# Products of probabilities and V in the tiles of the scores: two batches a product, and outputs that share two banks with the turned q and k

## The reference, cut to what matters

```python
scale, shift = split(emb @ W_emb + b_emb)
xn = rms_norm(x, g_norm) * (1.0 + scale) + shift
q, k, v = heads(xn @ W_qkv)                 # 16 heads of 16 channels, 32 positions
q = rms_norm(q, g_q);  k = rms_norm(k, g_k)
attn = softmax(q @ k^T * 16 ** -0.5)        # 32 x 32 for each batch and head
o = attn @ v                                # the product that the change touches
x = x + (o + o @ W_out)
x = x + GRU(initial = cond, inputs = x)     # 32 steps, one after the other
```

## Time and profile before

| | |
|---|---|
| time, median of 3 runs | 345.14 us (343.35 to 345.91) |
| the profiled execution | 347.7 us, of which its span is 345.5 us |
| mean granted TensorE clock | 0.995 |
| stretch of 18 even turns of the attention | 65.4 to 156.4 us of the span |
| the GRU's steps | from about 198 us to the end |

### The profile page before, as it was taken

How to read it: one execution, slowest core, us unless ns; L and a number is a source line. 1 busy time by engine, 2 the same in 40 slices (tenths; PEclk the granted TensorE clock), 3 DMA queues, 4 the chain that set the end, 5 groups by cost and what they waited for, 6 DMA issues and landing times.

```text
span 345.5 us, 12266 instructions
## 1 busy us (share of the span) xinstructions
PE 327.8 (95%) x4182; PEld 296.1 (86%) x4182; DVE 251.4 (73%) x665; ACT 237.3 (69%) x721; POOL 224.2 (65%) x403
## 2 busy tenths in 40 slices
PE   8998879999999999999976999999999999999994
PEld 7767667888888888888865999999999999999994
DVE  2768859999999999999987366655556566665555
ACT  3778767788787888888655566666666666666662
POOL 5688667687787778779965345555555555555552
PEclk9999989999999999999999999999999999999999
DMA  6885644334333332333342221121111111111111
GB/s 198 288 250 145 187 137 138 94 81 122 117 115 95 118 102 80 116 115 104 110 121 69 68 71 47 61 64 61 61 51 56 46 60 61 61 61 61 61 59 35
DMA packets 32199, 34.06 MB, mean 99 GB/s; under 512 B 5286, under 2 KB 26796, under 8 KB 32172
## 3 DMA queue, kind: packets, MB, share of 16 engines
q1 hardware_dynamic: 26108, 26.30, 25.4%
q10 hardware_dynamic: 6064, 7.41, 6.7%
HBM read 12.46 MB, written 8.39 MB: 60 GB/s over the span
## 4 chain that ended last, share of the span: by engine, by line
PE 82%; SPq 8%; ACT 2%; DVE 2%; DMA 2%; issue 2%; POOL 1%; DVEq 0%; POOLq 0%; ACTq 0%
PE bank L1206 38%; PE bank L1163 20%; PE bank L1336 5%; PE bank L1317 4%; SPq L394 4%; PE bank L1305 4%; SPq L402 4%; PE bank L1436 3%; PE bank L1169 2%; DMA operands<-operands 2%; PE bank L1288 2%; PE bank L1297 2%; PE bank L1183 1%; PE bank L1246 0%; DVE probsT L1042 0%
## 5 line engine op out<-in xcount | busy, mean ns | idle before, releaser
L1206 PE MATMUL bank<-wih_lo,wo_parts 128*128 128x256 f32 x192 | 56.3, 294 | 0.0
L1206 PE MATMUL bank<-wih_hi,wo_parts 128*128 128x256 f32 x192 | 53.7, 281 | 0.0
L1206 PE MATMUL bank<-wih_hi,pair_lo 128*128 128x256 f32 x192 | 52.9, 280 | 0.0
L1206 PE MATMUL bank<-wqkv_hi,hT_hi 128*128 128x256 f32 x192 | 52.7, 293 | 0.0
L583 POOL TENSOR_TENSOR operands<-operands,h 128x128 f32<-128x128 f32 x64 | 29.6, 462 | 35.4 <-ACT operands L869 34.4
L1206 PE MATMUL bank<-wqkv_lo,hT_hi 128*128 128x256 f32 x192 | 50.1, 280 | 0.0
L1106 DVE TENSOR_TENSOR operands<-bank,operands 128x128 f32<-128x128 f32 x64 | 18.6, 291 | 39.8 <-ACT operands L866 39.8
L1163 PE MATMUL bank<-wqkv_hi,xn_hi 128*128 128x512 f32 (+1 forms) x124 | 46.6, 376 | 0.3 <-POOL xn_lo L505 0.3
L1206 PE MATMUL bank<-wqkv_hi,hT_lo 128*128 128x256 f32 x192 | 42.8, 279 | 0.0
L590 POOL TENSOR_TENSOR w_emb_sb<-h,w_emb_sb 128x256 f32<-128x256 f32 x31 | 22.7, 733 | 30.0 <-DVE h L1123 30.0
L1163 PE MATMUL bank<-wqkv_hi,xn_lo 128*128 128x512 f32 (+1 forms) x124 | 42.0, 338 | 0.0
(11 more groups left out here) (136 smaller groups left out, 984.7 us busy)
## 6 DMA issues: line engine op xcount, KB each, us to landing
v_diag<-v_rows SPq DMA_DIRECT2D x128, 34.0 KB, 1.9
operands<-operands SPq DMA_DIRECT2D x64, 64.0 KB, 2.0
operands<-operands SPq DMA_DIRECT2D x32, 128.0 KB, 2.1
out_dram<-x ACTq DMA_DIRECT2D x16, 256.0 KB, 2.5
w_emb_sb<-out_dram SPq DMA_DIRECT2D x32, 128.0 KB, 2.1
out_dram<-w_emb_sb SPq DMA_DIRECT2D x31, 128.0 KB, 1.7
x_in<-in_x_dram SPq DMA_DIRECT2D x7, 512.0 KB, 9.0
stage_w<-in_L_cond_W_ih_dram ACTq DMA_DIRECT2D x2, 384.0 KB, 4.8
```

Of the source, the lines that this page charges most:

```text
L1206: return pe.matmul(dst, moved, gate_columns(weights, k, block), start=False, stop=True, skip_group_check=True)
```

## The change

The products of probabilities and V are cut into the tiles of the scores: 64 rows by 32 columns, two batches in each, so 32 products of 34 columns in place of 16 of 68. Row half i writes to `o_tiles[i]`, and the two are in different banks. To find a second bank for them, the outputs share two banks (`p_ko`) with the turned q and k: each bank holds one half of the turned q and k in its first 256 columns and the outputs of two batches behind them. Since ScalarE copies the turned q and k out of the banks from which VectorE reads the outputs, `reciprocals` now also waits until `queries_keys` of the group that was turned in the same TensorE turn is done (`qkT_ready`), and `attention_products` waits for the copy of the turn before. The readers' access patterns get one dimension more (the bank). The GRU's gate banks move accordingly: reset and update gates of the odd steps to `p_ko`, new gates to the two banks of the scores; so the new gate's bank of step 0 is cleared, set and filled one turn later than the others.

```diff
--- before.py
+++ after.py
@@ -157,14 +157,19 @@
 
         r_g, z_g, rh, npre, n_g, zh, zn = (gru_tile(KC, P) for _ in range(7))
 
-        p_xTw, p_vx2, p_qkT = (bank(f"bank{i}") for i in range(3))
-        p_s = ctx.enter_context(nc.psum_tensor("bank3", [P, 2 * BANK], F32))
-        p_o = bank("bank5")
+        p_xTw, p_vx2 = (bank(f"bank{i}") for i in range(2))
+        p_ko = ctx.enter_context(nc.psum_tensor("bank2", [P, 2 * BANK], F32))
+        p_s = ctx.enter_context(nc.psum_tensor("bank4", [P, 2 * BANK], F32))
         p_qk2 = ctx.enter_context(nc.psum_tensor("bank6", [P, 2 * BANK], F32))
         p_qk = [p_qk2[:, BANK * i:BANK * i + BANK] for i in range(2)]
         p_xT, p_w = p_xTw[:, 0:D], p_xTw[:, D:2 * D]
         p_x2T, p_v = p_vx2[:, 0:D], p_vx2[:, D:2 * D]
         s_tiles = [p_s[:, BANK * i:BANK * i + D] for i in range(2)]
+        OW = GB // 2 * (HEADS // 4) * VW
+        qkT_tiles = [p_ko[:, BANK * i:BANK * i + D] for i in range(2)]
+        qkT_halves = p_ko[:, :].rearrange("p (i f) -> p i f", i=2)[:, :, 0:D]
+        o_tiles = [p_ko[:, BANK * i + D:BANK * i + D + OW] for i in range(2)]
+        o_heads = p_ko[:, :].rearrange("p (i f) -> p i f", i=2)[:, :, D:D + OW].rearrange("p i (n f) -> p i n f", f=VW)
         s_heads = p_s[:, :].rearrange("p (i f) -> p i f", i=2)[:, :, 0:D].rearrange("p i (h k) -> p i h k", k=T)
 
 
@@ -237,6 +242,7 @@
         k_masked_ready = sem("k_masked_ready")
         k_diag_ready = [sem("k_diag_ready0"), sem("k_diag_ready1")]
         scores_clear = sem("scores_clear")
+        outputs_clear = sem("outputs_clear")
         square_x_free = sem("square_x_free")
         xhat_free = sem("xhat_free")
         s_ps = sem("s_ps")
@@ -326,8 +332,8 @@
 
 
 
-        rz_banks = [p.rearrange("p (c f) -> p c f", c=KC)[:, :, 0:2 * P] for p in (p_qk2[:, :], p_s[:, :])]
-        n_banks = [p_qkT, p_o]
+        rz_banks = [p.rearrange("p (c f) -> p c f", c=KC)[:, :, 0:2 * P] for p in (p_qk2[:, :], p_ko[:, :])]
+        n_banks = [p_s[:, BANK * i:BANK * i + BANK] for i in range(2)]
         hT_banks = [p_xTw[:, 0:P], p_vx2[:, 0:P]]
 
         def pair_index(base, n):
@@ -628,7 +634,7 @@
             act.wait_ge(qk_loaded[0], 16)
             act.copy(wqkv_hi[:, 0, 0:2 * D], stage_w[:, 0, 0:2 * D]).then_inc(wqk_hi_ready[0], 1)
             act.wait_ge(vec_ps, 1)
-            act.copy(vec_cols[:, :], p_o[:, 0:8]).then_inc(vec_cols_ready, 1)
+            act.copy(vec_cols[:, :], p_ko[:, 0:8]).then_inc(vec_cols_ready, 1)
 
             def shifts():
                 act.wait_ge(vec_cols_ready, 1)
@@ -686,9 +692,15 @@
                 for c in range(KC):
                     act.copy(hT_hi[:, c, :], condT[:, c, :]).then_inc(hi_ready[c], 1)
 
+            def set_reset_update(e):
+                act.copy(rz_banks[e].rearrange("p c (g a) -> p c g a", g=2), bias_sum).then_inc(rz_set, 1)
+
+            def set_new(e):
+                act.copy(n_banks[e].rearrange("p (i f) -> p i f", i=2), bias_n).then_inc(n_set, 1)
+
             def set_gates(e):
-                act.copy(rz_banks[e].rearrange("p c (g a) -> p c g a", g=2), bias_sum).then_inc(rz_set, 1)
-                act.copy(n_banks[e].rearrange("p (i f) -> p i f", i=2), bias_n).then_inc(n_set, 1)
+                set_reset_update(e)
+                set_new(e)
 
             def roots(n, nslot):
                 lo, hi = norm_columns(n)
@@ -723,7 +735,7 @@
                 if later(g, 2):
                     act.wait_ge(k_masked_ready, g - 1)
                     act.wait_ge(s_ps, g - 1)
-                act.copy(qkT[:, slot, :], p_qkT[:, :]).then_inc(qkT_ready, 1)
+                act.copy(qkT[:, slot, :].rearrange("p (i f) -> p i f", i=2), qkT_halves).then_inc(qkT_ready, 1)
 
             def exponentials(g, slot):
                 act.wait_ge(logits_ready, g + 1)
@@ -835,7 +847,10 @@
                 if turn_is(base, u, NG - 3 + ACT_OT):
                     act.wait_ge(bias_ready, 1)
                     act.wait_ge(gates_clear[0], 1)
-                    set_gates(0)
+                    set_reset_update(0)
+                if turn_is(base, u, NG - 2 + ACT_OT):
+                    act.wait_ge(gates_clear[0], 2)
+                    set_new(0)
 
             pipeline(act, body, NG - 1 + ACT_X2T)
 
@@ -1005,16 +1020,17 @@
                                   .broadcast_to([P, 2, HEADS // 2, T]),
                                   ALU.subtract).then_inc(logits_ready, 1)
 
-            o_heads = p_o[:, 0:GB * HEADS // 4 * VW].rearrange("p (n f) -> p n f", f=VW)
-
             def reciprocals(o, slot):
                 dve.wait_ge(o_ps, o + 1)
-                dve.reciprocal(inv_sum[:, slot, :], o_heads[:, :, DH]).then_inc(inv_ready, 1)
+                dve.wait_ge(qkT_ready, capped(o, PE_PV - PE_QKT + 1))
+                dve.reciprocal(inv_sum[:, slot, :].rearrange("p (i n) -> p i n", i=2), o_heads[:, :, :, DH])\
+                   .then_inc(inv_ready, 1)
 
             def attention_output(o, slot):
                 dve.wait_ge(inv_ready, o + 1)
-                dve.tensor_tensor(o_sb[:, slot, :].rearrange("p (n d) -> p n d", d=DH), o_heads[:, :, 0:DH],
-                                  inv_sum[:, slot, :].unsqueeze(2).broadcast_to([P, HEADS, DH]),
+                dve.tensor_tensor(o_sb[:, slot, :].rearrange("p (i n d) -> p i n d", i=2, d=DH), o_heads[:, :, :, 0:DH],
+                                  inv_sum[:, slot, :].rearrange("p (i n) -> p i n", i=2).unsqueeze(3)
+                                  .broadcast_to([P, 2, HEADS // 2, DH]),
                                   ALU.mult).then_inc(o_ready, 1)
 
             def modulated(g, slot):
@@ -1185,7 +1201,7 @@
                                          start=c == 0, stop=c == KC - 1)
                 last.then_inc(emb_ps, 1)
             pe.wait_ge(vec_loaded, 16 * 4)
-            pe.transpose(p_o[:, 0:8], vec_rows[:, :], ident[0:8, 0:8]).then_inc(vec_ps, 1)
+            pe.transpose(p_ko[:, 0:8], vec_rows[:, :], ident[0:8, 0:8]).then_inc(vec_ps, 1)
             keep_busy(p_qk[1], 12)
 
             def projection_input(slot):
@@ -1302,7 +1318,7 @@
                 if later(g, 1):
                     pe.wait_ge(qkT_ready, g)
                 for m in range(2 * KC):
-                    last = pe.transpose(p_qkT[:, m * P:m * P + P], qkn[:, slot, m * P:m * P + P], ident[:, :])
+                    last = pe.transpose(qkT_tiles[m // KC][:, m % KC * P:m % KC * P + P], qkn[:, slot, m * P:m * P + P], ident[:, :])
                 last.then_inc(qkT_ps, 1)
 
             def scores(g, slot):
@@ -1323,18 +1339,22 @@
             def attention_products(g, slot, place):
                 pe.wait_ge(probsT_ready, g + 1)
                 pe.wait_ge(v_diag_ready[place], spread_by_four(g, place, GB))
+                pe.wait_ge(qkT_ready, capped(g, PE_PV - PE_QKT))
                 if later(g, 1):
                     pe.wait_ge(o_ready, g)
+                pe.sem_inc(outputs_clear, 1)
                 for hq in range(HEADS // 4):
                     for j in range(4):
 
                         c, e = hq // 2, hq % 2
                         head = HC * c + 2 * j + e
                         column = HC * (j // 2) + NB * c + 2 * e + (0, 1, 1, 0)[j]
-                        dst = p_o[32 * j:32 * j + 32, 0:GB * HEADS // 4 * VW]\
-                            .rearrange("p (b n f) -> p b n f", b=GB, f=VW)[:, :, hq, :]
-                        last = pe.matmul(dst, probsT[:, slot, column, :], v_diag[:, place, :, head, :],
-                                         start=True, stop=True)
+                        for i in range(2):
+                            rows = slice(2 * PB * i, 2 * PB * i + 2 * PB)
+                            dst = o_tiles[i][32 * j:32 * j + 32, :]\
+                                .rearrange("p (b n f) -> p b n f", b=GB // 2, f=VW)[:, :, hq, :]
+                            last = pe.matmul(dst, probsT[rows, slot, column, :],
+                                             v_diag[rows, place, 2 * i:2 * i + 2, head, :], start=True, stop=True)
                 last.then_inc(o_ps, 1)
 
             def output_projection(g, slot):
@@ -1384,16 +1404,21 @@
                 if turn_is(base, u, NG + PE_QKT):
                     pe.wait_ge(qkn_ready, NG)
                     pe.wait_ge(qkT_ready, NG)
-                    unread_products([rz_banks[0][:, 0, :], rz_banks[0][:, 1, :]], 3)
-                    clear_gates(0).then_inc(gates_clear[0], 1)
+                    unread_products([rz_banks[0][:, 0, :], rz_banks[0][:, 1, :]], 4)
+                    unread_products([rz_banks[0][:, 0, :], rz_banks[0][:, 1, :]], 2).then_inc(gates_clear[0], 1)
+                if turn_is(base, u, NG + 1 + PE_QKT):
+                    pe.wait_ge(logits_ready, NG)
+                    unread_products([n_banks[0][:, :]], 1).then_inc(gates_clear[0], 1)
                 if turn_is(base, u, NG + 2 + PE_QKT):
                     pe.wait_ge(rz_set, 1)
+                    for k in range(KC):
```

(9 more changed lines are left out.)

## The result

The changed kernel takes 353.52 us (median of 4 runs, 353.23 to 353.85) where the kernel before takes 345.14 (4 runs, 343.35 to 345.91). The ratio is 1.0236, with an interval from 1.0208 to 1.0263. The forecast was 344.3 and its range ended at 349.3. The profiled execution of the changed kernel took 353.36, with a span of 351.1. Two executions of this study (350.09 us of the kernel before and 354.15 of the run "cut in the loop alone") fell in a slower state, and no ratio uses them.

The account below looks back on a forecast made before the run. TensorE was taken as the bound, VectorE less than 0.35 us behind. Even turns -1.0, entry +0.3 and end -0.15 made -0.85 us, so 345.14 became 344.3, range 341.3 to 349.3.

Parts of the forecast that it names:

- eight starts at 7 ns take 0.053, so the starts set the pace: 64 x 6.7 ns = 0.43 us: TensorE's 32 small products: 64 records start at the pace seen over eight starts, 0.43 us in all.
- the 13 that the forecast had named as the sign of being wrong: TensorE's small products: 13 ns a record in the changed kernel would show the forecast wrong.
- The other bound, 27 ns a product: TensorE's small products at the pace of the scores' whole group: 0.87 us for 32, a turn 0.24 longer.
- rival 2: TensorE's small products are issued no faster than the scores' products: 0.24 us more a turn, 350 us; chance 0.13.
- The ring: VectorE's sum of squares, ScalarE's roots and copies, VectorE's `reciprocals` onward, closed by the new wait: 5.00 us a turn.
- sum of squares to the end of the copy: From the start of VectorE's sum of squares to the end of ScalarE's copy: 10.06 us over four turns.
- signal to `reciprocals`: Hand-over from ScalarE's copy to VectorE: 0.05 us a turn, bounds 0 to 0.12.
- `reciprocals` to `modulated`: On VectorE, from the start of `reciprocals` to that of `modulated`: 0.20 us a turn.
- `modulated` to the next sum: On VectorE, from `modulated` to the next sum of squares: 8.87 us over four turns.
- TensorE idle in every turn: Even turns: TensorE has idle time for the first time, some 0.15 us a turn.
- +0.3 and -0.15: Outside the 18 even turns: 0.3 us lost at the loop's entry before them, 0.15 us gained behind them.
- falls away after the last turned group: Behind the even turns, from 156 us on: the wait for the copy ends after the last turned group.

Follow-up runs that it names:

- cut in the loop alone: Kernel before with each of the 16 products cut in two on the same tile and bank, only in the loop's 20 turns: 348.89 us, ratio 1.0081.
- half the products: Changed kernel with 16 of its 32 products, two of four batches left out for each head from the second group on: 346.79 us, ratio 1.0034.
- the wait in the loop alone: Kernel before with `reciprocals` also waiting for ScalarE's copy of q and k, only in the loop's 20 turns: 347.50 us, ratio 1.0056.
- the wait alone: Kernel before with only one addition, `reciprocals` of every group also waiting for ScalarE's copy of q and k: 348.58 us, ratio 1.0103.
- the second profile of before: Kernel before run once more, unchanged, for another profile: 345.22 us.
- the products first: Changed kernel with ScalarE's store behind its copy of q and k, and TensorE's products with V ahead of the scores: 352.30 us, ratio 1.0179.

## Why the prediction was wrong

**The pace of the products.** The step that failed is "eight starts at 7 ns take 0.053, so the starts set the pace: 64 x 6.7 ns = 0.43 us", and with it "Eight starts at 7 ns speak for the fast end, and I take it". The starts 7 ns apart are real, and up to 32 records go out so fast behind long instructions. They are not sustained: 0.78 us for 64 behind the scores, and 0.75 with half the columns. That is 12 ns a record, near the 13 that the forecast had named as the sign of being wrong. The other bound, 27 ns a product from the group of scores, was near (24). It was the only pace that the trace of before showed over a whole group, and I set it aside for one seen over eight records. In TensorE's turn it makes +0.16 for -0.20 (+0.13 with the mean of 0.75), which decides the sign: rival 2 is what happened, at a chance of 0.13, and its own sum of 350 was still too low, because beside the longer turn it gave the wait 0.3 us at the loop's entry and no more. The rule of the Trainium skill named there ("TensorEngine Tiling (Array Packing)", section Instruction Overhead), that a short matmul costs as much as one of some 60 columns, gave an estimate of 0.80; behind the scores the trace agrees (0.78, and 0.75 with half the columns) if a product, and not each of its two records, is counted as a matmul, and behind long instructions it does not for the first 16 products (0.17 us).

**The ring.** The mechanism was right: `reciprocals` waits for the copy in every turn, the idle time moved there, and the store's turn is the latest. Its sizes were low. The run with half the products allows the comparison term by term over four turns (sums of squares at 94.87, 100.24, 105.17, 110.27 and 115.19; the rows above show one of these turns, the same two views have the others):

| term, four turns | forecast | measured |
|---|---|---|
| sum of squares to the end of the copy | 10.06 | 2.79 + 2.33 + 2.51 + 2.33 = 9.96 |
| signal to `reciprocals` | 0.20 | 0.09 + 3 x 0.10 = 0.39 |
| `reciprocals` to `modulated` | 0.80 | 0.28 + 0.22 + 0.28 + 0.28 = 1.06 |
| `modulated` to the next sum | 8.87 | 2.21 + 2.28 + 2.21 + 2.21 = 8.91 |
| together | 19.93 | 20.32 |

20.32 is 5.08 a turn, more than the old 5.055. So with the products as fast as I had them the kernel comes to about 346.8 (346.3 by its ratio to the runs of before beside it) and not to 344.3. The two terms that no row of before showed for this place, the signal and the start of `modulated` behind `reciprocals`, are the ones that were short. I had taken both nearer to their low ends than to their high ones: 0.05 of 0 to 0.12, and 0.20 of 0.16 to 0.37.

**Where the two are together.** In the changed kernel TensorE's 5.21 sets three turns of four, and the store's turn takes 5.58 (95.47 to 101.05): four turns are 21.18 for 20.22. The forecast had TensorE idle in every turn; it is idle in one of four.

**Ahead of and behind the even turns.** The forecast had +0.3 and -0.15; it was +1.6 and +2.5. I had written that the wait "falls away after the last turned group"; it still stands for the groups before, in turns with less work on TensorE, and the run with the wait in the loop alone has 1.5 less than the wait alone from group 25 to group 31. "The last products gain some 0.1" fell with the pace: they lost. In the changed kernel the products of group 31, the last, start 4.64 us after its scores, in the second profile of before 3.96. Which part of these 4 us is the products, which the wait, and which the longer code or SyncE's issues (10% of the chain for 8%) was not separated: the differences are near the 1 us by which unchanged stretches differ.

**What stays open.** That the number of small products sets their time, and not their columns, is shown, and that a first group of them goes out faster behind long instructions or after a wait. What sets the pace behind it, the fetching of instructions, their decoding or the weight load that each product has, was not tried. Nor was any run made with the shared banks or the readers' extra dimension alone; the run with half the products bounds them only together with the wait.

## What to carry to other kernels

Price small products by the pace of a whole group behind the same kind of work, never by the distances inside a burst; halving the columns of products of 68 columns while doubling their number was a loss here (0.46 us became 0.67 on the same tiles). A wait that joins two engines' chains has to be summed turn by turn with every hand-over in it (here 0.10 for a signal, and 0.28 to the next instruction), and here it decided in the one turn of four in which something else stood ahead of the signal: moving a store's issue behind the copy took 1.4 us of the wait's 1.7 in the loop. Cut a profile into stretches and profile the kernel before twice; the 18 looped turns agreed to 0.02 us, the start only to 3.

## What the runs showed that I had not expected

In the kernel with the products first, behind long instructions, they go out in a burst of about 32 records in 0.17 us, and then at 12 ns a record with pauses (0.40 us for the next 32). Behind the scores, which are 16 short products themselves, the burst is only about half as long: up to 101.70 there are 17 records, the last of which starts 0.32 - 0.19 = 0.13 us after the first, and all 64 take 0.78.

```profile
101.51 0.32 PE L1356 MATMUL bank<-v_diag,probsT 64*32 64x34 f32 x17
```

In the changed kernel's group 5, where TensorE had waited for VectorE first, the burst is the long one again, here in a window that ends at 59.05:

```profile
58.87 0.36 PE L1356 MATMUL bank<-v_diag,probsT 64*32 64x34 f32 x32 [0.80 <-DVE probsT L1058]
```
